# Two steps' weighted values computed back to back in the last stage of an attention kernel

## The reference, cut to what matters

```python
x = x + attn(einsum('bct,bcd->bdt', x, cond_weights[idx]))   # x: 64 batches, 32 tokens, 512 features
x = x + ffn(cond2(x))

# attn: 32 heads of 128; q, k, v = h @ W + b; q and k are rms-normalised over all 4096 columns
attn = softmax(q @ k.T / sqrt(128)); out = attn @ v; return out @ Wo + bo

# cond2: x @ w_eff.T, with w_eff made from weight, scale_log, codebook and lora_B @ lora_A
# ffn: 8 experts of rank 16, weighted by a softmax over router logits
low = einsum('bsd,hrd->bshr', x, A)
out = 2 * einsum('bshr,hor,bsh->bso', low, B, 8 * softmax(x @ Wr.T + br))
```

## Time and profile before

| | us |
|---|---|
| median of three runs | 1520.62 |
| the profiled execution | 1523.46 |
| its span | 1521.7 |
| TensorE busy, matmuls | 1500.4 (99%) |
| TensorE busy, weight loads | 1270.9 (84%) |
| VectorE busy | 1044.3 (69%) |
| ScalarE busy | 729.1 (48%) |
| GpSimd busy | 753.6 (50%) |

### The profile page before, as it was taken

One profiled execution on the slowest core, in us unless ns is written; L12 is line 12 of the kernel. 1 busy time (PEld: TensorE's weight loads), 2 busy tenths in 40 slices (PEclk: granted clock), 3 DMA queues, 4 the chain that ended last, 5 costly groups with the idle time before them and its releaser, 6 DMA issues.

```text
span 1521.7 us, 37231 instructions
## 1 busy us (share of the span) xinstructions
PE 1500.4 (99%) x15638; PEld 1270.9 (84%) x15638; DVE 1044.3 (69%) x1528; ACT 729.1 (48%) x1328; POOL 753.6 (50%) x531
## 2 busy tenths in 40 slices
PE   9999999999999999998999999999999999999998
PEld 8777888888888888887999999998887878878876
DVE  7667666676666767664498888977676666666663
ACT  6666666667667666665323333334342222222221
POOL 6477777777777877775344444443451111111100
PEclk9999999999999999999999999999999999999998
DMA  3111011110111100111534443356455243343330
GB/s 144 56 43 33 32 43 43 42 44 29 36 43 43 43 30 35 43 43 36 158 114 139 139 132 130 127 167 207 162 167 153 85 140 101 96 134 93 109 98 29
DMA packets 105912, 134.74 MB, mean 89 GB/s; under 512 B 6017, under 2 KB 88065, under 8 KB 105233
## 3 DMA queue, kind: packets, MB, share of 16 engines
q1 hardware_dynamic: 105280, 132.23, 26.5%
q10 hardware_dynamic: 464, 0.13, 0.0%
HBM read 86.20 MB, written 46.14 MB: 87 GB/s over the span
## 4 chain that ended last, share of the span: by engine, by line
PE 92%; DVE 5%; ACT 1%; issue 1%; DMA 1%; POOL 0%; SPq 0%; DVEq 0%; ACTq 0%; POOLq 0%
PE bank L560 40%; PE bank L756 22%; PE bank L569 19%; PE bank L714 4%; PE bank L655 3%; PE bank L824 1%; PE bank L794 1%; DMA wraw<-score_spill 1%; DVE accr L1385 1%; PE bank L525 1%; DVE qreg L1384 0%; PE bank L545 0%; DVE xs_lo L1350 0%; DVE ot L1566 0%; PE bank L550 0%
## 5 line engine op out<-in xcount | busy, mean ns | idle before, releaser
L560 PE MATMUL bank<-xs_hi,wa 128*128 128x512 f32 x1792 | 574.1, 395 | 3.4 <-ACT snap L949 1.2
L1204 POOL TENSOR_TENSOR accr<-accr,sqst 128x512 f32<-128x512 f32 x248 | 353.1, 1433 | 174.0 <-ACT sqst L961 123.5
L560 PEld LDWEIGHTS bank<-xs_hi,wa 128*128 128x128 f32 x1792 | 336.4, 188 | 79.5 <-issue 4.5
L560 PE MATMUL bank<-xs_lo,wa 128*128 128x512 f32 x896 | 349.0, 389 | 0.0
L569 PE MATMUL bank<-wv,xs_hi 128*128 128x256 f32 x1792 | 325.0, 284 | 6.0 <-DVE wv L1297 3.5
L756 PE MATMUL bank<-ot,wo_main 128*128 128x512 f32 x1344 | 321.8, 395 | 0.5 <-issue 0.5
L756 PEld LDWEIGHTS bank<-ot,wo_main 128*128 128x128 f32 x1344 | 247.8, 188 | 54.3 <-issue 0.6
L569 PEld LDWEIGHTS bank<-wv,xs_hi 128*128 128x128 f32 x1792 | 280.3, 192 | 9.1 <-DVE wv L1297 4.1
L569 PE MATMUL bank<-wv,xs_lo 128*128 128x256 f32 x896 | 254.0, 284 | 0.0
L1289 DVE TENSOR_TENSOR wa<-wraw,wa 128x256 fp32r<-128x256 f32 (+1 forms) x160 | 134.3, 840 | 131.3 <-ACT wa L874 130.0
L1049 ACT ACTIVATE ot<-bank,vec 128x256 fp32r<-128x256 f32 x256 | 100.3, 474 | 235.4 <-PE bank L714 235.4
(11 more groups left out here) (186 smaller groups left out, 1725.8 us busy)
## 6 DMA issues: line engine op xcount, KB each, us to landing
sqst<-v_spill SPq DMA_DIRECT2D x63, 512.0 KB, 4.0
wraw<-in_wqk SPq DMA_DIRECT2D x32, 512.0 KB, 3.5
v_spill<-vo SPq DMA_DIRECT2D x64, 256.0 KB, 2.3
v_spill<-sqst SPq DMA_DIRECT2D x64, 256.0 KB, 2.3
score_spill<-sqst SPq DMA_DIRECT2D x32, 256.0 KB, 2.0
wraw<-in_wv SPq DMA_DIRECT2D x16, 512.0 KB, 5.1
wraw<-score_spill SPq DMA_DIRECT2D x16, 512.0 KB, 5.8
accr<-in_wo SPq DMA_DIRECT2D x16, 512.0 KB, 5.3
```

The source lines that it names most:

```text
L560: ins = pe.matmul(dst[:, :], wa[:, col:col + P], xpart[:, j - 1, kt, n * CH:(n + 1) * CH], start=(first and k == 0), stop=(k == 5), skip_g ...
L1204: pool.tensor_tensor(a, a, sq_slot(count), ALU.add).then_inc(acc_done, 1)
```

## The change

TensorE's loop goes over pairs of steps. For each even `b` from 2 it issues `pv(b)`, `pv(b + 1)`, `project_out(b - 1)`, then a wait for `out_lo(b)`, then the router's or experts' matmuls that fall on the pair, and then `project_out(b)`. `pv(0)` and `pv(1)` both go into the last step of the value stage. Odd steps get their own two PSUM banks, 6 and 7, so `pv(b)` waits for `out_lo(b - 2)` in place of `out_lo(b - 1)`. The router's and experts' results go to banks 4 and 5, which adds waits to some `pv`: at `p` = 4 for `keep_low`, at `p` = 8 for `keep_lowt`, at `p` = 10 and 12 for `add_expert`, and once, at step 6, for `low_keep`.

VectorE now transposes for step `b + 2` after `out_lo(b)` (before: for `b + 1` ahead of it). The softmax parts move: `shift` and the exponential to `b % 4 == 3`, `invert` and `normalise` to `b % 4 == 0`, `scale_scores` to `b % 4 == 2`, `load_scores` to `b % 4 == 1`. Wo's low part of step 0 is computed by GpSimd, no longer by VectorE, and `load_v(1)` and `load_wo(1)` go one step of the value stage earlier.

```diff
-        pv_bank = (bank[4], bank[5])
+        def pv_bank(b, r):
+            return bank[4 + 2 * (b % 2) + r]
...
-                if s == N_ST - 1:
+                if s == N_ST - 2:
                     sp.wait_ge(w_eff_done, 2)
+                    load_v(1)
                     load_wo(1)
-                    load_v(1)
...
-                if b % 4 == 3 and b // 4 + 2 < NG:
+                if b % 4 == 1 and b // 4 + 2 < NG:
                     load_scores(b // 4 + 2)
...
-                if c >= 1 and p in (9, 10, 11, 12):
+                if c >= 1 and p in (10, 12):
+                    store_out(c - 1, p - 10)
                     store_out(c - 1, p - 9)
...
             def pv(b):
...
-                if b >= 1:
-                    pe.wait_ge(o_lo, 2 * b)
-                else:
+                c, p = b // NP, b % NP
+                if b >= 2:
+                    pe.wait_ge(o_lo, 2 * b - 2)
+                elif b == 0:
                     pe.wait_ge(c21_done, N_ST - 1)
                     pe.wait_ge(c12_done, N_ST - 1)
+                else:
+                    pe.wait_ge(c11_done, N_ST - 1)
+                    pe.wait_ge(lora_used, 4)
+                if b == 6:
+                    pe.wait_ge(low_ready, 2)
+                if c >= 1 and p == 4:
+                    pe.wait_ge(rl_kept, 2 * c)
+                if c >= 1 and p == 8:
+                    pe.wait_ge(lowt_done, c)
+                if c >= 1 and p in (10, 12):
+                    pe.wait_ge(fin_done, KI * (c - 1) + p - 8)
...
                     pv(0)
+                    pv(1)
...
-            for b in range(STEPS):
+            project_out(0, (3, 2, 0, 1))
+            for b in range(2, STEPS, 2):
                 c, p = b // NP, b % NP
-                if b == 1:
-                    project_out(0, (3, 2))
-                    pv(1)
-                    project_out(0, (0, 1))
-                elif b >= 2:
-                    pv(b)
-                    project_out(b - 1)
-                if b in (4, 6):
-                    low_product(b // 2 - 2)
+                pv(b)
+                pv(b + 1)
+                project_out(b - 1)
+                pe.wait_ge(o_lo, 2 * b + 2)
+                if b == 4:
+                    low_product(0)
+                    low_product(1)
                 if c >= 1:
-                    if p in (2, 3):
-                        low_rank(c - 1, p - 2)
+                    if p == 2:
+                        low_rank(c - 1, 0)
+                        low_rank(c - 1, 1)
                     if p == 6:
                         transpose_low(c - 1)
-                    if p in (8, 9, 10, 11):
+                    if p in (8, 10):
                         expert(c - 1, p - 8)
+                        expert(c - 1, p - 7)
+                project_out(b)
             project_out(STEPS - 1)
...
                 if r == 0 and b == 1:
+                    act.wait_ge(p_done[3], N_ST)
...
-                if b % 4 == 0 and b // 4 + 1 < NG:
-                    q = b // 4 + 1
-                    act.wait_ge(sm_shift, q + 1)
-                    act.activation(sc[q % 2], sc[q % 2], ACT.Exp).then_inc(sm_exp, 1)
-                if b in (4, 6):
-                    low_keep(b // 2 - 2)
+                if b == 0:
+                    exponent(1)
+                if b % 4 == 3 and b // 4 + 2 < NG:
+                    exponent(b // 4 + 2)
+                if b == 5:
+                    low_keep(0)
+                    low_keep(1)
                 if c >= 1:
                     if p == 4:
                         expert_exp(c - 1)
-                    if p == 6:
+                    if p == 7:
                         keep_lowt(c - 1)
...
+            low_o(0)
             for b in range(STEPS):
...
+                if b == 1:
+                    normalise(1)
+                if b % 4 == 2 and b // 4 + 2 < NG:
+                    scale_scores(b // 4 + 2)
+                if b % 4 == 0 and b >= 4 and b // 4 + 1 < NG:
                     normalise(b // 4 + 1)
-                if b % 4 == 3 and b // 4 + 2 < NG:
-                    scale_scores(b // 4 + 2)
...
                 c, p = b // NP, b % NP
-                if 1 <= b < STEPS - 1:
-                    transpose_p(b + 1)
                 if b >= 1:
                     out_lo(b, 0)
                     out_lo(b, 1)
                 if c >= 1 and p == 0:
                     residual(c - 1)
-                if b % 4 == 0 and b // 4 + 1 < NG:
-                    shift(b // 4 + 1)
-                if b % 4 == 1 and b // 4 + 1 < NG:
+                if b + 2 < STEPS:
+                    transpose_p(b + 2)
+                if b == 0:
+                    shift(1)
+                if b == 1:
+                    invert(1)
+                if b % 4 == 3 and b // 4 + 2 < NG:
+                    shift(b // 4 + 2)
+                if b % 4 == 0 and b >= 4 and b // 4 + 1 < NG:
                     invert(b // 4 + 1)
                 if c >= 1:
                     if p == 3:
                         keep_low(c - 1, 0)
-                    if p == 4:
                         keep_low(c - 1, 1)
                         logits(c - 1)
-                    if p == 5:
+                    if p == 4:
                         expert_scores(c - 1)
-                    if p in (9, 10, 11, 12):
+                    if p in (9, 11):
                         add_expert(c - 1, p - 9)
+                        add_expert(c - 1, p - 8)
```

More of the change, by code:

```diff
@@ L712, in pv @@
                                 rows = slice(r * 64, (r + 1) * 64)
-                                out = pv_bank[r][d * 64:(d + 1) * 64, (h * TC + t) * 64:(h * TC + t + 1) * 64]
+                                out = pv_bank(b, r)[d * 64:(d + 1) * 64, (h * TC + t) * 64:(h * TC + t + 1) * 64]
                                 ins = pe.matmul(out, values(b)[rows, t, h * DH + d * 64:h * DH + (d + 1) * 64],
@@ L760, in project_out @@
                         ins.then_inc(o_sum, 1)
-                    elif i == (1 if b == 0 else KI - 1):
+                    elif i == outputs[-1]:
                         ins.then_inc(o_done, 1)
@@ L766, in low_product @@
                 pe.wait_ge(ld_awr, 16)
[L767 to L770, removed]
                 for i in (2 * half, 2 * half + 1):
@@ L773, in low_product @@
                         at = (ob % 2) * D + i * P
-                        ins = pe.matmul(bank[7][:, (i % 2) * LR:(i % 2 + 1) * LR], qf[ob // 2][:, at:at + P],
+                        ins = pe.matmul(bank[4 + half][:, (i % 2) * LR:(i % 2 + 1) * LR], qf[ob // 2][:, at:at + P],
                                         awr_sb[:, ob, :], start=(ob == 0), stop=(ob == KI - 1))
@@ L780, in job_bank @@
             def job_bank(c, k):
-                return bank[(7, 4, 5, 6, 7, 4, 5)[k]] if c == NCH - 1 else bank[7]
+                return bank[(7, 4, 5, 6, 7, 4, 5)[k] if c == NCH - 1 else (4, 5, 4, 4, 5, 4, 5)[k]]
             def low_rank(c, half):
                 pe.wait_ge(res_done, KI * (c + 1))
[L785 to L791, removed]
+                pe.wait_ge(low_ready, 2)
                 for t in (2 * half, 2 * half + 1):
@@ L1101, in low_keep, with exponent @@
                 act.wait_ge(low_raw, half + 1)
-                act.activation(lowmat[:, 2 * half:2 * half + 2, :], bank[7][:, 0:2 * LR].rearrange("p (i n) -> p i n", i=2),
+                act.activation(lowmat[:, 2 * half:2 * half + 2, :], bank[4 + half][:, 0:2 * LR].rearrange("p (i n) -> p i n", i=2),
                                ACT.Copy).then_inc(low_ready, 1)
+            def exponent(q):
+                act.wait_ge(sm_shift, q + 1)
+                act.activation(sc[q % 2], sc[q % 2], ACT.Exp).then_inc(sm_exp, 1)
             def expert_exp(c):
@@ L1112, in keep_lowt @@
                     act.wait_ge(fin_raw, KI * c)
-                act.activation(low_t, (bank[5] if c == NCH - 1 else bank[7])[:, :], ACT.Copy).then_inc(lowt_done, 1)
+                act.activation(low_t, bank[5 if c == NCH - 1 else 4][:, :], ACT.Copy).then_inc(lowt_done, 1)
             for b in range(STEPS):
@@ L1553, in transpose_p @@
                 ins.then_inc(pt_ready, 1)
-            def low_o():
-                dve.wait_ge(wo_hi, 1)
-                dve.tensor_tensor(wo_slot(0)[:, 1, :], wo_raw[0], wo_slot(0)[:, 0, :].bitcast(F32), ALU.subtract)\
-                   .then_inc(wo_lo, 1)
             def out_lo(b, r):
@@ L1565, in out_lo @@
                 for h in range(2):
-                    ins = dve.scalar_tensor_tensor(out=ot_part(ot[:, b % 2, 1, h, :], r), in0=pv_part(r, h),
+                    ins = dve.scalar_tensor_tensor(out=ot_part(ot[:, b % 2, 1, h, :], r), in0=pv_part(b, r, h),
                                                    scalar=vec[:, 2 * (b % NP) + h, 2:3],
@@ L1605, in _ @@
                     transpose_p(0)
-                    low_o()
-                if u == 31:
                     transpose_p(1)
@@ L1622, in keep_low @@
```

(4 more changed lines are left out.)

13 lines of the change are left out of this document (4 added, 9 removed).

## The result

The changed kernel takes 1534.56 us, the median of four runs (1531.60 to 1535.13), against 1520.62: the ratio is 1.0085, with a 95% interval of 1.0066 to 1.0105. The forecast was 1526.7, with 1517 to 1531 as its range. The direction was right; the slowdown is 13.9 us and not 6.1. Run once more beside the experiments, the same kernel had the ratio 1.0091 (1.0075 to 1.0106).

The account below looks back on a forecast made before the run. TensorE's instruction order was taken as the bound (busy 99%). Stalls 17.5 less seams 12.2 and old waits 2.6 gave +2.7 us; the clock's 3.4 made +6.1, on the median 1520.62: 1526.7 us, 8-in-10 range 1517 to 1531.

Parts of the forecast that it names:

- The seams: TensorE's passages into and out of 64x64 matmuls: 32 fewer at 0.38 us each, 12.2 us less.
- The old waits: TensorE's waits for out_lo(1) and at chunk boundaries go: 2.6 us less together.
- What is late next: Odd steps' chain from out_hi to transpose_p, with work inserted into it, makes TensorE wait: stalls of 17.5 us.
- p = 8: pv waits for keep_lowt, behind shift and the exponential: 2.7 us in each of three chunks, 8.1 us.
- p = 12: pv waits for two add_expert that stand behind shift: 1.1 us, two times, 2.2 us.
- p = 0: residual between out_lo and transpose_p delays the next pair's second pv: 1.2 us, three times, 3.6 us.
- the start: First steps of the last stage: TensorE waits ahead of pv(3) for a late transpose_p(3), 3.6 us.
- The clock: TensorE's granted clock falls to half after idle times near three us: two falls of a possible four, 3.4 us.
- The stalls without the clock: Rival: the new stalls come but no fall of TensorE's clock: +2.7 us, 1523.3 us; chance 0.20.
- A shorter odd chain: Rival: the odd steps' chain is 1.2 us shorter than walked, stalls fall to some 7 us: 1513; chance 0.14.
- Dear seams: Rival: a pair's second pv pays most of the passage again, saving only 7.4 us: 1531.5; chance 0.06.
- No stall at p = 8: Rival: keep_lowt gets its turn on ScalarE ahead of the exponential, so pv doesn't wait: 1516.6 us; chance 0.03.

Follow-up runs that it names:

- the version without stalls: Changed kernel with keep_lowt, add_expert, keep_low, logits, shift(1), exponential(1), the residual's loads and one invert reordered: 1510.44 us, ratio 0.9931 to the kernel before.

## Why the prediction was wrong

**The bound, right.** TensorE's order is the time: the difference of the stages comes out of its waits, its passages and its clock.

**The seams, right.** 0.38 us for a passage from the rows, 0.40 measured between two kernels that differ in nothing else. The lower bound (0.23) is out.

**The old waits, right as far as seen.** 2.6 us. Together with the seams 14.8 were forecast; the version without stalls shows 12.3 + 2.2 = 14.5 in its stage.

**What is late next, right in all nine places, and a tenth was missed.** In waiting time p = 8 has 2.6 (2.7 walked), p = 12 1.0 (1.1), p = 0 0.9 (1.2), the start 3.1 (3.6). The sentence that failed is "Each pair's two loads of values have 11 us": it left out that SP issues `load_res(0)` and `load_res(1)` at step 14, behind a wait for GpSimd, and ahead of `load_v(17)`, which had 6.7 us. That is 2.6 us of waiting at the first chunk boundary which no term of the sum had, and a fall with it. The queue was walked for the scores and not for this boundary.

**The clock, the step that failed.** "I take two falls of a possible four": five came in the profiled execution, and four in the one of the second timing. Read from the starts of TensorE's rows, a fall cost 1.5 to 1.6 us beside the undisturbed passage over the same work, 7.8 us for the five and not 3.4. The mechanism was right and was confirmed by extra matmuls in the same stall; the term was mis-sized. One of the five stands behind the wait that wasn't forecast, four behind the four that were. Both falls of the trace before went with idle times of 2.9 us, and I counted those of 2.7 as even chances. In the profiles of the changed kernel and of the experiments, 22 of 28 idle times between 2.5 and 3.2 us in this stage had a fall that began within 1.5 us of their end, and none of 1.9 us or less did.

The stages give the sum. I compare the starts of the 31 pairs with those of the version with all causes moved, whose only waits are the 2.2 us at the start. So measured, the stalls are three of 2.7, two of 1.05, three of 1.1, 3.1 at the start and 2.7 for the load: 19.3 us, where 17.5 were walked. 19.3 - 14.5 + 7.8 = 12.6, and the stages differ by 479.1 - 467.5 + 0.94 = 12.5. Of the 6.4 us above the forecast's 6.1, the clock is 4.4, the stalls are 1.8 (the load 2.7, the others 0.9 less than walked) and the smaller gain is 0.3.

**From the stage to the median.** Outside the stage the profiled execution was 1.4 us ahead of this sum (1.07 in front of it, 0.36 in the tail), so it stands at 1534.6 where 1529.6 was forecast. The forecast then took off 2.84 us, by which the kernel before's profiled execution was above its median. The changed kernel's profiled execution is at its median (1534.62 and 1534.56). So 2.8 of the 7.9 us that the median is off come from that step: one execution compared with one, of kernels whose executions differ by several us.

**The rivals.** The stalls without the clock: out, since the clock fell. A shorter odd chain: out, it is 8.45 us against 8.4. Dear seams: out by the two kernels with and without pairs. No stall at p = 8: out; but what it described, `keep_lowt` ahead of the exponential, is the edit that alone wins the whole slowdown back.

## What to carry to other kernels

Two units issued back to back save a passage, and make the second unit's consumers wait for all that was put between: walk the later one's chain through every engine and every place where something is inserted, and walk the DMA queue over the same places. In this kernel a wait of TensorE of 2.5 to 3.2 us cost more than its length: in 22 cases of 28 a fall of the clock came with it, some 1.5 us on top. Cutting such a wait, or filling it with matmuls that nobody reads, was worth it by itself. Put short work that gates TensorE ahead of work that has to wait for another engine: `keep_lowt` had its input long before, and stood behind an exponential that waited for VectorE's `shift`. That one line's order on ScalarE was 14 us.

## What was not expected of the hardware

- Work that nobody needs made the kernel faster: six extra matmuls at three places, 6.7 us; eleven at two places, 4.3 us on one kernel and 2.5 on another.
- Idle times of the same length did not always bring the fall: 2.62 us ahead of p = 8 did in two chunks and not in the third in one profile, and 3.19 us at a chunk boundary did not. The idle time of 2.9 us near 700, which the change doesn't touch, had a fall in nine of the eleven profiles without extra matmuls there, and none in the other two. Single executions of one kernel differ by several us: the twelve with VectorE's order changed spread over 6.6 us, the fastest at a mean granted clock of 0.997 and the slowest at 0.992.
- With two loads of values and two of 1 MB issued within 7 us, the last of the values landed 9 us behind its issue; the median of such loads is 5.3 us in that profile and 4.0 in the kernel before.
